# Two scatters of an expert block without a wait between them, and the destinations computed three parts later

## The reference

```python
for e in range(E):                                  # E = 8 experts, F = 1024
    w_tok = mult1 * (idx[:, 0] == e) + mult2 * (idx[:, 1] == e)
    h = jax.nn.silu(x @ w1[e].T) * (x @ w3[e].T)
    out = out + w_tok[:, None] * (h @ w2[e].T)
```

## Time and profile before

| what | us |
|---|---|
| median of 3 runs (lowest, highest) | 1797.75 (1795.05, 1801.78) |
| the profiled execution: time, span | 1796.06, 1794.3 |
| TensorE busy | 1566.2 (87%) |
| VectorE busy | 1128.1 (63%) |
| ScalarE busy | 900.5 (50%) |
| GpSimd busy | 757.1 (42%) |
| 64 scatters L1461, busy, mean | 100.0, 1.562 |
| a load of weights, median to landing | 11.7 |

### The profile page before, as it was taken

How to read it: one execution, slowest core, us unless ns; L and a number is a source line. 1 busy time by engine, 2 the same in 40 slices (tenths; PEclk the granted TensorE clock), 3 DMA queues, 4 the chain that set the end, 5 groups by cost and what they waited for, 6 DMA issues and landing times. The chain is left out here.

```text
span 1794.3 us, 46494 instructions
## 1 busy us (share of the span) xinstructions
PE 1566.2 (87%) x17664; PEld 1195.9 (67%) x17664; DVE 1128.1 (63%) x2617; ACT 900.5 (50%) x2175; POOL 757.1 (42%) x920
## 2 busy tenths in 40 slices
PE   4899999984999999999999999829999999999991
PEld 2677777763566666666666666518898898898891
DVE  4566666662888788778888888634444444444443
ACT  2344455442466666666666666604444443443444
POOL 6334444322755556765676567421121111121112
PEclk9999999997799999999999999959999999999996
DMA  6666776634455545554554455167776766766744
GB/s 178 180 188 187 194 195 186 193 113 99 136 139 142 149 138 136 164 153 136 141 161 145 134 154 153 49 224 250 245 267 215 245 228 228 246 216 229 260 143 173
DMA packets 205508, 318.92 MB, mean 178 GB/s; under 512 B 61000, under 2 KB 174056, under 8 KB 205288
## 3 DMA queue, kind: packets, MB, share of 16 engines
q1 hardware_dynamic: 183784, 249.78, 45.3%
q0 software_dynamic: 21504, 66.19, 12.6%
HBM read 224.52 MB, written 91.03 MB: 176 GB/s over the span
## 5 line engine op out<-in xcount | busy, mean ns | idle before, releaser
L1154 DVE TENSOR_REDUCE cross_mx<-cross_bank_max 112x2 f32<-112x750 f32 x512 | 460.2, 931 | 115.4 <-PE cross_bank_max L1273 113.1
L985 ACT ACTIVATE cross_probs<-cross_bank_score 125x448 f32<-125x448 f32 x768 | 406.2, 545 | 238.2 <-PE cross_bank_score L1263 235.4
L1461 POOL DMA_INDIRECT acc<-experts_y,experts_dest_i x64 | 100.0, 1562 | 459.4 <-DMA acc<-experts_y,experts_dest_i 260.6
L1263 PE MATMUL cross_bank_score<-cqst,ckst 97*125 97x448 f16 x768 | 282.7, 370 | 4.7 <-ACT cross_probs L985 2.4
L1273 PE MATMUL cross_bank_max<-ckst,cqst 96*112 96x375 f16 x1024 | 257.5, 334 | 28.8 <-DVE cross_mx L1154 21.1
L1538 DVE TENSOR_TENSOR experts_hid<-experts_bank_h,experts_gated 128x256 f32<-128x256 f32 (+1 forms) x288 | 113.4, 394 | 245.2 <-ACT experts_gated L1487 240.2
L1572 PE MATMUL experts_bank_h<-experts_x_hi,w 128*128 128x256 f16 (+1 forms) x1536 | 239.1, 267 | 22.3 <-DVE experts_hid L1538 20.9
L1289 PE MATMUL cross_bank_out<-cross_probs,cross_val 125*32 125x112 f32 x6144 | 201.6, 264 | 0.1
L1572 PE MATMUL experts_bank_h<-experts_x_lo,w 128*128 128x256 f16 (+1 forms) x768 | 198.9, 267 | 0.0
L1273 PEld LDWEIGHTS cross_bank_max<-ckst,cqst 96*112 96x112 f16 x1024 | 128.9, 133 | 89.1 <-DVE cross_mx L1154 36.3
L1487 ACT ACTIVATE experts_gated<-experts_bank_h 128x256 f32<-128x256 f32 (+1 forms) x288 | 103.1, 358 | 155.2 <-PE experts_bank_h L1572 152.5
(11 more groups left out here) (245 smaller groups left out, 3045.1 us busy)
## 6 DMA issues: line engine op xcount, KB each, us to landing
w<-w_halves SPq DMA_DIRECT2D x24, 3072.0 KB, 11.8
experts_w_third<-w_halves SPq DMA_DIRECT2D x12, 3072.0 KB, 11.7
cross_ew<-in_experts POOLq DMA_DIRECT2D x32, 768.0 KB, 5.6
w_halves<-cross_ew_half POOLq DMA_DIRECT2D x32, 768.0 KB
ckst<-cross_k SPq DMA_DIRECT2D x96, 187.5 KB
cross_v<-front_v SPq DMA_DIRECT2D x24, 531.2 KB
cross_val<-cross_v SPq DMA_DIRECT2D x32, 398.4 KB
front_src<-in_ctx_t SPq DMA_DIRECT2D x24, 500.0 KB, 6.0
```

The source lines that it names most:

```text
L985: nc.scalar.activation(probs[:, e % PROBS], bank_score[e % 2][0:SC, 0:4 * T], ACT.Exp, scale=CROSS_SCALE).then_inc(probs_ready, 1)
L1154: nc.vector.tensor_reduce(mx[:, b % nb, 2 * n:2 * n + 2], bank_max[n % 2][0:T, :, 0:S], AX.X, ALU.max).then_inc(max_read, 1)
L1263: nc.tensor.matmul(bank_score[e % 2][0:SC, 0:pair_w], kst[:, p, g, k * SC:(k + 1) * SC], qst[:, p, g, :], start=True, stop=True).then_inc( ...
```

## The change

On GpSimd, the wait of a block's second scatter for the landing of the first is taken out. The wait for the scatters of the block before stays, and stands now ahead of the loop over the tiles. On VectorE, the call of `destinations(j)` moves from part f = 2 to part f = 5 of the block, behind `x_low(j + 1)`.

```diff
                 for j in range(BLOCKS):
                     p = j % 2
                     wait(pool, meta_done, j + 1)
+                    wait(pool, y_stored[1 - p], 16 * slot_tiles_before(j, 1 - p))
                     for i in range(tiles(j)):
                         wait(pool, y_ready, tiles_before(j) + i + 1)
-                        if i:
-                            wait(pool, y_stored[p], 16 * (slot_tiles_before(j, p) + i))
-                        else:
-                            wait(pool, y_stored[1 - p], 16 * slot_tiles_before(j, 1 - p))
                         pool.indirect_dma_start(acc[:, :], bass.IndirectOffsetOnAxis(ap=dest_i[:, p, i:i + 1], axis=0),
                                                 y[:, p, i], None, compute_op=ALU.add).then_inc(y_stored[p], 16)
...
                         if f:
                             h_low(j, f - 1)
-                        if f == 2:
-                            destinations(j)
                         if f == 4 and on(j + 1):
                             x_low(j + 1)
+                        if f == 5:
+                            destinations(j)
```

## The result

The changed kernel takes 1768.76 us (median of 4 runs, 1767.2 to 1769.9), the kernel before 1799.76 us beside it (1795.05 to 1802.02): a ratio of 0.9836, with a 95% interval of 0.982 to 0.9852. It is faster by 1.6%. The forecast was 1769.5 us, in a range of 1763 to 1785 us. The profiled execution has a span of 1767.3 us against 1794.3 us.

A forecast was written before the change was run, and what follows sets the result against it. The prediction took TensorE's idle time and lost clock in the expert stage, from late scatters behind small blocks, as the recoverable bound. Terms -30.4 + 3.5 - 0.8 = -27.7 us gave 1769.5 us, range 1763 to 1785 us.

The forecast's parts named there:

- The wait chain: Expert stage: scatter, destinations, hid, TensorE wait in turn behind seven small blocks; removing this saves 30.4 us.
- The second scatter lands 9.3 to 15.2 us behind its start: GpSimd, block 11: started at 1397.03, the second scatter lands between 1406.3 and 1412.2, taken as some 1408.
- The upper end: Block 11's second scatter moves only once the first has landed at 1404.5, takes 7.7 us more and lands at 1412.2.
- Either edit alone would nearly do: Expert stage: old wait at f = 5 is 1.2 us late and absorbed; new landing at f = 2 is 0 to 4.4 us late.
- Each small block pays 0.5 us: VectorE in seven small blocks: destinations at f = 5 delays the last h_low, TensorE waits 0.5 us each, +3.5 us.
- Nothing for the rows: SyncE's row loads behind small blocks: issued later but still in time, margin 0.9 us, cost 0 us, bounds 0 and 7 x 1 us.
- The tail gives 0.8 us: End of the expert stage: the last scatter starts 0 to 1.5 us sooner, counted as -0.8 us.
- half a stall that stays: Rival, expert stage: two scatters beside a 3 MB load land too late, half of 30.4 us stays, 1784 us; chance 0.11.
- rows with a delay of their own: Rival, behind small blocks: rows need 8.0 to 9.2 us from issue regardless, costing 8 to 16 us, about 1782 us; chance 0.10.
- no change: Rival, expert stage: VectorE's wait goes but TensorE finds another of the same size, 1796 us; chance 0.05.
- The slower one: Rival, SyncE loads: rows mix with the next weights, TensorE stands 5.9 us seven times and loses clock, 1824 us; chance 0.06.

The follow-up runs named there:

- the other two: Second scatter not waiting for the first, destinations at f = 2, against the kernel before: two row buffers 1835.61 us in one run, three row buffers 1835.3 us.

## Why the prediction was right, point by point

- *The wait chain costs 30.4 us and all of it goes.* Shown. The stretch fell by 26.83 us with 7 x 0.48 = 3.4 us of new cost in it, so 30.2 us went, idle time and clock both. Three kernels take the stall away, each by another link of the chain: the scatter edit alone, the move alone, and the weights left out. The prediction gave 20.17 and 19.02 us as the length of a large block behind a small one; the seven run from 18.6 to 21.8 us. Its sum doesn't use these two.
- *The second scatter lands 9.3 to 15.2 us behind its start, likely some 11 us.* Measured 9.6 to 11.2 us. The upper end, one scatter moved after the other, did not come about: the pair needs 11.9 us where two by themselves needed 9.3 us and another 8.4 us. The prediction called that end the nearer one by the rule of the Trainium skill on rings in order ("DMA: Bandwidth & Descriptors", Queues, rings and completion order). That rule says in which order descriptors are taken, and not that a transfer waits for the landing of the one before; the prediction read the second into it. That two in flight share most of their waiting fits the 11.9 us, but no run shows what they wait for beyond the weights.
- *Either edit alone would nearly do.* Shown, with 463.26 us and 464.76 us. With the move alone VectorE waits 0.4 to 2.4 us, under the 2.9 us that TensorE absorbs, and in block 13 0.7 us where the prediction had 1.2 us. With the scatter edit alone VectorE doesn't wait at all, where it allowed 0 to 4.4 us.
- *Each small block pays 0.5 us for `destinations` at f = 5.* Measured 0.48 us, and gone in both kernels that have `destinations` at f = 2 in small blocks. The bounds were 0.2 and 0.9 us; on another chip it was 9.21 - 8.52 = 0.7 us. The one wait of 0.5 us forecast for a block shows as three short ones of the weight loads, for parts 5, 6 and 7.
- *Nothing for the rows.* Right in the changed kernel, and in part by luck: in the tightest block they land just as their turn begins (issued at 1336.81, 6.9 us, turn at 1343.70), and 1.2 us ahead in block 13. The prediction worked its margin out for block 13. In the block of 9.2 us before, the rows landed at 1336.02 + 9.2 = 1345.22 and this was their turn, 0.27 us later, so that + 0.5 - 0.96 us gives a wait of 0.2 us and no margin:

```profile
1345.49 0.60 PE L1558 MATMUL experts_bank_x<-experts_ident,experts_rows 128*128 128x128 f32 x4
```

Where `destinations` stays at f = 2 in small blocks and the rows have two buffers, they are late. With the scatter edit alone it is by up to 0.6 us, and 2.0 us are taken back. Two things are in it, and their shares are not shown. The small block is 0.48 us shorter there. And the rows land later behind the weights ahead of them: in block 13 those took 11.8 us, as in the changed kernel (11.7 us), but the rows landed 13.9 us behind their issue (1391.21 + 9.9 - 1387.23) and not 12.6 us. The weights' longer median (12.4 us in place of 11.7 us, and 11.9 us with the move alone) goes with two scatters in flight, but does not explain that block. So of the 3.5 us that the move costs, the scatter edit alone wins only 1.5 us.
- *The tail gives 0.8 us.* The term that was mis-sized. From the issue at the end of block 32 to the end of the kernel these are the windows of before and after:

```profile
1716.03:1794.30 78.27, 39.89 (x413) 36.12 (x410) 31.02 (x127) 32.43 (x85) 19.43 (x26) 0.78 0.45 148
```

```profile
1689.29:1767.30 78.01, 39.90 (x413) 36.15 (x410) 31.01 (x127) 32.45 (x85) 19.43 (x26) 0.78 0.45 149
```

78.27 and 78.01 us: 0.3 us, in one execution each. The start of the last scatter was forecast rightly. This is its row in the changed kernel:

```profile
1730.51 1.55 POOL L1458 DMA_INDIRECT acc<-experts_y,experts_dest_i  x1 [4.90 <-ACT experts_y L1495]
```

The first load of `finish`, the phase behind, in the kernel before and in the changed one:

```profile
1765.43 1.94 SPq L1612 DMA_DIRECT2D finish_r<-acc  x4
```

```profile
1738.58 2.13 SPq L1609 DMA_DIRECT2D finish_r<-acc  x4
```

It starts 41.22 us behind the issue at the end of block 32, 0.8 us sooner than before (1758.01 - 1716.03 = 41.98 us). But that load goes 49.29 us behind the same issue instead of 49.40 us. What failed is the step from a sooner scatter to a sooner end: from its start to that load it is 8.07 us instead of 7.42 us. All nine profiled executions with the scatter edit have 8.0 to 8.2 us there, the move alone 7.6 us. Why is open.

Of the rivals, half a stall that stays, rows with a delay of their own, and no change are refuted by the stretch. The slower one had the engines mix rows and weights issued close together. The rows of block 14 land at 1399.7, with the next weights issued 2.0 us behind them and landing 12.8 us after that, at 1408.8; so they are not mixed in. The loads in the other order show only what late rows cost, by another mechanism.

## What to carry to other kernels

When one engine's wait shows up as another's, count both: seven waits against seven waits named the chain, and the difference of their sums (41.5 and 20.9 us) gave the slack, 2.9 us a time, that let the move alone suffice though VectorE still waited. Before moving a block of small instructions later in a row, look for the shortest iteration: the place cost nothing in the large blocks and 0.5 us in each of seven small ones. A load that is needed soon should be issued ahead of the big one in its queue. Issued 4.5 us ahead (before) or 2.0 us ahead (after), the rows landed 0.5 to 0.9 us behind the weights that were already under way.

## What the runs showed of the hardware that I had not expected

- Two accumulating scatters in flight beside a 3 MB load land 9.6 to 11.2 us after the second one's start, 0.3 to 1.9 us later than one by itself (9.3 us, block 11 before). Without the load one lands 1.55 + 3.0 us after its start.
- The same kernels took some 70 us more on two other chips (1871.58 and 1870.6 against 1801.68 us for the kernel before), with the 32 expert blocks nearly the same. The traces of the scatter edit alone on two chips are alike up to 600 us; from 600 to 800 us the slower chip has 2210 matmul records in place of 2496, at a granted clock of 0.97 in place of 1.00. The changed kernel was 15 us behind the other two on one of them, in all of its four runs; in its profiled execution 10 us of that lie ahead of the experts, with a clock of 0.94 to 0.95 from 600 to 1000 us. Why is open.
